# Adding x on TensorE and copying on ScalarE in a fused state-space and mixture-of-experts block, with some waits of VectorE reordered

## What is computed

```python
x = x + mamba(ln_channels(x))          # pixel_shuffle(2): 4 x 2304 tokens of width 128 in sequence
t = to_tokens(x)                       # 2304 tokens of width 512
t = t + moe(ln_tokens(t))              # 8 experts, the best 2 of each token, and one shared expert

# mamba, per token of the sequence (256 inner channels, 16 states)
u, z = split(seq @ in_proj_w.T);  u = silu(causal_conv4(u) + conv_b)
dt, B, C = split(u @ x_proj_w.T);  dt = softplus(dt @ dt_proj_w.T + dt_proj_b)
h = exp(dt * A) * h + (dt * u) * B     # per channel and state, a recurrence over the sequence
y = sum_n(h * C) + u * D;  out = (y * silu(z)) @ out_proj_w.T

# shared expert, width 1024, added like the routed experts
shared = (silu(tn @ sw1) * (tn @ sw3)) @ sw2
```

## Time and profile before

| | |
|---|---|
| median of three runs | 2363.06 us |
| the profiled execution, its own time | 2365.38 us |
| its span, first to last instruction | 2363.6 us |
| PE busy | 2116.5 us (90%) |
| DVE busy | 1298.8 us (55%) |
| POOL busy | 1219.8 us (52%) |
| ACT busy | 1038.7 us (44%) |

### The profile page before, as it was taken

The page is one execution under the profiler, slowest core; times in us unless marked ns, Lnnn a source line. Parts: engine busy times, 40 slices in busy tenths (PEclk is TensorE's granted clock), DMA queues, the critical chain, the costliest instruction groups (busy, mean ns, idle before and its releaser), DMA issues.

```text
span 2363.6 us, 30197 instructions
## 1 busy us (share of the span) xinstructions
PE 2116.5 (90%) x8172; PEld 1141.4 (48%) x8173; DVE 1298.8 (55%) x2036; ACT 1038.7 (44%) x2114; POOL 1219.8 (52%) x1132
## 2 busy tenths in 40 slices
PE   5667778989889899898878999999999999999995
PEld 4223335555555555555446844444444444444443
DVE  2799999999989999999983411111111111111112
ACT  3787788877778777887732111101101101101100
POOL 3699998999889999899870001111111111111110
PEclk8678789999989999999989999999999999999996
DMA  5555655556545565555635231413132313141116
GB/s 191 145 143 142 160 141 139 145 136 155 149 129 137 143 155 144 142 144 140 159 93 197 90 120 19 132 27 125 26 93 61 130 27 126 24 133 22 23 22 169
DMA packets 156887, 271.71 MB, mean 115 GB/s; under 512 B 16800, under 2 KB 103944, under 8 KB 154192
## 3 DMA queue, kind: packets, MB, share of 16 engines
q1 hardware_dynamic: 147120, 247.61, 36.5%
q0 software_dynamic: 9632, 22.55, 5.2%
HBM read 222.58 MB, written 51.71 MB: 116 GB/s over the span
## 4 chain that ended last, share of the span: by engine, by line
PE 56%; issue 11%; ACT 10%; DVE 8%; POOL 8%; DMA 6%; SPq 1%; POOLq 0%; ACTq 0%; DVEq 0%
PE pair L1836 21%; PE single L1848 13%; PE pair L1557 7%; DVE WALL L1269 6%; POOL WALL L710 4%; DMA u<-xrows,gix 3%; PE pair L1563 3%; ACT WALL L993 2%; PE single L1475 2%; PE pair L1676 2%; ACT L796 1%; DMA WALL<-yrows 1%; POOL sp L608 1%; PE single L1512 1%; PE pair L1819 1%
## 5 line engine op out<-in xcount | busy, mean ns | idle before, releaser
L710 POOL TENSOR_TENSOR WALL<-WALL 128x768 f32<-128x768 f32 x384 | 694.6, 1814 | 50.9 <-DVE WALL L1269 39.3
L1269 DVE TENSOR_TENSOR_SCAN WALL<-WALL,carry,pair 128x384 f32<-128x384 f32 x640 | 610.2, 992 | 0.0
L1836 PE MATMUL pair<-WALL,zz 128*128 x1376 | 597.8, 592 | 2.0 <-ACT zz L1093 1.1
L993 ACT ACTIVATE WALL<-WALL,AnR 128x384 f32<-128x384 f32 x768 | 425.3, 605 | 48.1 <-DVE WALL L1269 32.6
L771 POOL DMA_INDIRECT yrows<-sp,aix x43 | 68.9, 1601 | 688.7 <-ACT sp L1105 671.0
L1836 PEld LDWEIGHTS pair<-WALL,zz 128*128 128x128 f32 x1376 | 258.1, 190 | 311.0 <-issue 311.0
L1423 DVE SCALAR_TENSOR_TENSOR sp<-XA,tab,pair 128x512 f32<-128x512 f32 x86 | 64.3, 747 | 567.0 <-ACT XA L1099 567.0
L1557 PE MATMUL pair<-XA,WALL 128*128 128x288 f32 x1024 | 298.1, 442 | 48.3 <-ACT XA L908 39.9
L1848 PE MATMUL single<-WALL,sp 128*128 x688 | 303.1, 593 | 2.7 <-issue 1.5
L1099 ACT ACTIVATE XA<-pair 128x512 f32<-128x512 f32 x86 | 51.4, 597 | 577.6 <-PE pair L1836 577.6
L1557 PEld LDWEIGHTS pair<-XA,WALL 128*128 128x128 f32 x1024 | 205.0, 205 | 127.3 <-issue 43.6
(11 more groups left out here) (262 smaller groups left out, 2261.2 us busy)
## 6 DMA issues: line engine op xcount, KB each, us to landing
WALL<-dtd SPq DMA_DIRECT2D x384, 192.0 KB, 3.9
WALL<-in_L_ffn_w_dram SPq DMA_DIRECT2D x24, 2048.0 KB, 13.8
WALL<-wsd SPq DMA_DIRECT2D x144, 256.0 KB, 3.2
WALL<-crows SPq DMA_DIRECT2D x96, 192.0 KB, 4.1
dtd<-sp SPq DMA_DIRECT2D x96, 192.0 KB, 2.8
WALL<-wsd SPq DMA_DIRECT2D x16, 768.0 KB, 4.6
X<-in_x_dram SPq DMA_DIRECT2D x4, 1152.0 KB, 6.5
xrows<-rows SPq DMA_DIRECT2D x24, 192.0 KB, 2.8
```

Source lines behind the costliest of these rows:

```text
L710: pool.tensor_tensor(hC[m], hs[:, (NS * j + n) % HRING, :, :], Cs[k][:, n % NPH // 2, :].unsqueeze(1).to_broadcast([P, HALF, T]), ALU.mult ...
L993: a = nsc.activation(dA[(NS * j + n) % AHEAD][:, e, :], dtR[:, h * NQ + c + e, :], ACT.Exp, scale=AnR[:, c + e, h, q:q + 1])
L1269: scan = nv.tensor_tensor_scan(hs[:, m, e, :], dA[(NS * j + n) % AHEAD][:, e, :], dBu[e], init, ALU.mult, ALU.add)
L1836: last = mm(bank[2 * w + q][:, :], xT[k][:, r, :], WALL[:, ds(off + (w * RR * I + r * I + q * 512), 512)], start=(r == 0), stop=(r == RR - 1))
```

## The change

In the Y step TensorE adds x by an identity product at the end of the second piece of each row block (`down_piece` with the image), and the sum is copied over x: three of four copies by ScalarE at n = 6, 10 and 14 of its list, the last by VectorE at n = 12. Two H1 copies of ScalarE move: the first from n = 3 to n = 2, ahead of the table load there, the fourth from n = 9 into `exps` at n = 7, ahead of its second table load. On VectorE the residue and the gate products move behind the scans of their n. At the start GpSimd runs the softplus tail of the first chunk ahead of the centring of the third, with half 0 of `dt*u` ahead of half 1 of `dt`, and SP stores and spreads `dt` and `dt*u` half by half. In `softplus_tail` each half of `dt*u` waits for its own half of `dt`.

```diff
+        H1_INSIDE = (0, 3)
         GATED_AT = (0, 2, 4, 6, 8, 10, 12, 14)
-        Y_OUT = (1, 5, 9, 12)
+        Y_OUT = (6, 10, 14)
+        Y_LAST = 12
...
             for h in range(HALF):
                 store_dt(0, 0, h)
                 spread_dt(0, 0, h)
-            for h in range(HALF):
                 store_dtu(0, 0, h)
                 spread_dtu(0, 0, h)
...
                     if h == 0:
-                        pool.wait_ge(f_dt, HALF * (g + 1))
                         pool.wait_ge(f_u, 2 * g + 2)
+                    pool.wait_ge(f_dt, HALF * g + h + 1)
                     pool.tensor_tensor(dtu[:, h, :], dt[:, h, :], u[k][:, h, :], ALU.mult).then_inc(f_dtu, 1)
...
             low_part(0, 0)
+            for n in (3, 4, 7, 5, 6, 8):
+                softplus_tail(n, 0, 0)
             front_centre(2, 0, 2)
-            for n in range(NS):
-                softplus_tail(n, 0, 0)
...
-            def exps(g, with_exp=None, with_ln=None):
+            def exps(g, with_exp=None, with_ln=None, shared_group=None):
...
                 nsc.activation(onex[:, :, :], onex[:, :, :], ACT.Copy, bias=-1.0).then_inc(f_e1, 1)
+                if shared_group is not None:
+                    h1_copy(shared_group, H1_INSIDE[1], E1)
                 exp_and_ln()
...
-                                if phase == H1_OUT[q] // NS and n == H1_OUT[q] % NS:
+                                if q not in H1_INSIDE and phase == H1_OUT[q] // NS and n == H1_OUT[q] % NS:
                                     h1_copy(G, q, E1)
+                            if phase == 2 and n in Y_OUT:
+                                y_to_x(G, b - 1, j // GC, Y_OUT.index(n), E1)
                         if n == 2:
...
                             if not first and j % GC == 1:
                                 shared_silu(group_of(b, j))
+                            if not first and j % GC == 0:
+                                h1_copy(group_of(b, j), H1_INSIDE[0], E1)
                             exp_and_ln()
...
-                            exps(g + 1)
+                            exps(g + 1, shared_group=group_of(b, j) if not first and j % GC == 0 else None)
...
-                        if front and n == 1:
-                            residue(g + 1, 1 - k)
-                        if not first and j % GC == 1 and n in GATED_AT:
-                            shared_gate(group_of(b, j), GATED_AT.index(n), E1)
-                        if not first and j % GC == 2 and n in Y_OUT:
-                            r = Y_OUT.index(n)
-                            v.wait_ge(e_ps, 3 * PH * group_of(b, j) + 2 * PH + 2 * r + 2)
-                            xv = xgroup(b - 1, j // GC, r)
-                            nv.tensor_tensor(xv, xv, E1, ALU.add).then_inc(e_y, 1)
                         v.wait_ge(m_dA, i + 1)
...
                             scan.then_inc((m_h0, m_h)[e], 1)
+                        if front and n == 1:
+                            residue(g + 1, 1 - k)
+                        if not first and j % GC == 1 and n in GATED_AT:
+                            shared_gate(group_of(b, j), GATED_AT.index(n), E1)
+                        if not first and j % GC == 2 and n == Y_LAST:
+                            v.wait_ge(e_ps, 3 * PH * group_of(b, j) + 3 * PH)
+                            nv.tensor_copy(xgroup(b - 1, j // GC, RR - 1), E1).then_inc(e_y, 1)
...
-                    down_piece(w, half, q, E1)
+                    down_piece(w, half, q, E1, b)
```

## The result

The changed kernel takes 2335.22 us (median of 4 runs, 2332.33 to 2339.89) against 2363.03 (4 runs, 2360.93 to 2366.53): a ratio of 0.9883, 95% interval 0.9863 to 0.9903. It is 27.8 us faster; 48.3 were forecast, 2315 us, with a range of 2294 to 2340. The profiled execution took 2339.89 us, 25.5 less than that of before. VectorE's first pair comes 8.5 us earlier and its last one, n = 15 of step 23, 26.2 us earlier (1202.42 instead of 1228.57), so the whole difference lies in the recurrence, as the prediction had it.

A forecast was written before the change was run, and what follows sets the result against it. VectorE was taken to set the recurrence's pace, with GpSimd and TensorE nearly full. Terms 20.9 - 2.5 - 12.5 + 17.4 + 16 + 9.0 = 48.3 us off the profiled 2365.4, less 2.3 for the median: 2315 us, range 2294 to 2340.

The forecast's parts named there:

- the forecast case: Whole kernel: the summed terms hold, 2315 us, own range 2300 to 2328; chance 0.60.
- the rival of the bank that is not free in time: Y step: ScalarE's n = 10 copy comes late and stalls TensorE, 17 us in six groups, 2332 us; chance 0.18.
- the first product: Start: VectorE's first product was to come at about 64.4 us.
- the spread: Recurrence: VectorE was to idle under 8 us ahead of its products for the spread, instead of 21.4.
- Additions: VectorE: 24 additions of x and their waits go, 20.9 us; six copies give 2.5 back.
- The price on TensorE: TensorE: 24 identity products, about 0.5 us each, 12 us; hidden except three in a Y step.
- The last copy: Y step: VectorE's last copy of a group waits 2.5 us for TensorE, 12.5 us back in five groups.
- ScalarE's three copies: ScalarE at n = 6, 10, 14: 18 copies, 7.3 us, cost nothing if in time for the bank's reuse.
- Residue and gates: VectorE: placed behind the scans, waits of 10.7 and 6.7 us both go, 17.4 us; bounds 7 and 17.4.
- H1 copies: H1 steps: earlier ScalarE copies remove most of VectorE's spread wait, 16 us; bounds 8 and 21.4.
- The start: Start: earlier softplus tail and interleaved halves bring VectorE's start 9.0 us forward; bounds 6 and 9.
- the rival that GpSimd sets the pace: Loop at GpSimd's pace: VectorE's waits only change names; 2354 us (chance 0.04) or 2362 us (0.04).

The follow-up runs named there:

- p4_y: Kernel before the change with only x's additions replaced by the identity product and copies on ScalarE and VectorE: 2356.75 us, ratio 0.9964.
- q4_noident: Changed kernel without the loop's 24 identity products, so x is missing from the shared expert's sum in those groups: 2339.25 us, ratio 0.9884.
- r1_centre: Changed kernel with one GpSimd statement, the front norm's centring of the third chunk ahead, moved from n = 10 to n = 8: 2317.56 us, ratio 0.9794.
- p3_h1: Kernel before the change with only ScalarE's two H1 copies moved: 2363.99 us, ratio 0.9994.

## Why the prediction was right, and where its sizes were off

The direction, the place (the recurrence) and the range were right; the size was not, 27.8 us of 48.3. The measured time lies outside the forecast case's own range (2300 to 2328) and beside the rival of the bank that is not free in time (2332), which did not happen. It lies within the whole range because that was kept wide on the slow side, for GpSimd, which the prediction named and priced at nothing: the number was covered in part by luck. Of its signs the first product (64.92), the H1 step and the spread (1.9) came; the residue (9.5, not none), the gates (9.0, not almost none) and the last copies (22.4, not 12) did not. Term by term:

- **Additions** (20.9 us, less 2.5 for six copies). Right. The copy takes 453 ns, 0.45 where 0.42 was taken. Alone, with the wait of the last copy, they were to give 5.9 us, and *p4_y* gave 7.7.
- **The price on TensorE.** Right in size: 406 ns per instruction again, 1.5 us at the last copy by *q4_noident*. That the total would feel it was wrong.
- **The last copy** (12.5 us back). Right alone (10.4 in *p4_y*), wrong in the whole (22.4). The step that failed is "the three identity products ahead of its end add 1.5": in the Y step shown, the last piece starts 38.5 us into the step instead of 35.3 (926.98 in a step that began at 891.68), and of the 3.2 us only a part is identity products. The 1.91 us wait for `mcp` and the 1.5 us by which the piece behind it is slower were not in the sum.
- **ScalarE's three copies** ("they cost nothing as long as they are in time"). They were in time: TensorE waited for one of them once, 1.3 us. What the prediction left out is the mean copy that stands behind them in ScalarE's list; but the copies make only part of its lateness. In the step shown it starts 22.47 us into the step, 20.42 before and 20.73 in *p4_y*, which has the same copies and where TensorE waits for it 0.9 us at most. The rest comes with the other parts: ScalarE's table load in front of the step ends 0.2 us into it, and 1.4 us ahead of it before. That alone does not mend it: in *r1_centre* the load ends 1.4 us ahead again, but ScalarE then waits 2.15 us for TensorE's product of dt, and the mean copy starts at 22.30. By the rule of the Trainium skill (Perfetto Trace Analysis, Optimizing Tensor Performance, on matmuls), as the prediction read it, each copy would have lain bare between two pieces, 7.3 us; the trace has those 1.3 us.
- **Residue and gates** (17.4). Alone the edit took 13.4 us of these waits away, and 3.9 us came out at the end. In the whole change 18.5 us of waits stand there again: 1.9 us later is not late enough when what they want has itself become later.
- **H1 copies** (16). The wait went as forecast and further (21.4 to 1.9 us), the H1 step is clean, TensorE waits at most 1.4 us for an H1 copy instead of 5.2. Alone it gave nothing.
- **The start** (9.0). 8.5 us at the first product; alone 5.9 at the end, as the residue of step 0 took 1.9 of it.

The mis-sized step is one: the terms were added as if each wait stood for itself, with "nothing is taken off for GpSimd". And the rival that GpSimd sets the pace got 8 in 100, on the ground that "no idle time of VectorE ends with GpSimd". It does not, and still GpSimd held VectorE up, through ScalarE's square, then ScalarE's copies, then TensorE. The ledger of VectorE's idle time shows it: 49.6 us before and between 45.0 and 51.0 with any part alone, whichever wait the part removed, 42.8 with all four, and 23.5 with the centring moved as well. That rival's times (2354 and 2362) were too far on the other side, since the loop did not stand wholly at GpSimd's pace: the additions' own 10 us, the start and some of the waits did go. What share of *p3_h1*'s lost gain ScalarE's longer wait at the square (18.7 us more) explains by itself was not measured; the centring was moved only in the changed kernel.

## What to carry to other kernels

When several engines are each over 90% busy, a wait that is removed on the first is only a claim on slack in the others: before adding up removed waits, read the waits of every other engine, and look for one that nobody on the critical engine names but that a whole in-order list stands behind. Run each part alone and add up the idle time over all places: if the sum stays while its parts move, look for the common cause and stop mending places. And where two norms or copies share a helper's line, take the waiting one from the timeline, not from the group.

## What was not expected of the hardware

After a stop of 1.9 us TensorE ran the next piece at half its clock, although in the 35 us before the stop its only gap was 0.15 us: the window of that piece shows a granted clock of 0.55 (mostly the lower of the two levels, 1.2 GHz), and that of a piece in another Y step, one piece further on, 1.00 (columns as in the earlier trace rows).

```profile
897.74:901.53 3.79, 3.79 (x10) 2.21 (x8) 3.79 (x6) 3.79 (x12) 3.61 (x4) 0.55 0.59 145
609.12:611.33 2.21, 2.21 (x13) 1.79 (x10) 2.21 (x4) 0.00 (x0) 2.21 (x3) 1.00 0.86 235
```

So a stop of 1.9 us was followed by another 1.5 us lost, almost as much again. Most such stops show it, not all: behind the four stops of 1.9 us in the changed kernel's Y steps the piece took 3.2 to 3.8 us, behind the fifth, of 1.6 us, 2.10; in *r1_centre* one of four stops of 1.9 us was followed by 2.10 too, the others by 3.1 to 3.6. On GpSimd, four instructions over 96 columns take 1.42 us where one over all 384 takes 1.00 (24.2 against 17.0 us in 17 steps): cutting an operation there costs 0.14 us per further piece.
